# A gated attention and mixture-of-experts block: the passage from the GRU to the experts without GpSimd arithmetic

## The reference

```python
x = x + tanh(g_xattn[0]) * xattn(layernorm(x), ctx, ...)      # 3 GRU iterations
h = layernorm(x)
scores = sigmoid(h @ gate_w.T)
topk_score, topk_ids = top_k(scores.T, cap)
xin = h[topk_ids]
eo = (silu(xin @ gw + gb) * (xin @ up_w + up_b)) @ down_w + down_b
out = zeros.at[topk_ids].add(eo * topk_score)
shared = (silu(h @ sh_gate) * (h @ sh_up)) @ sh_down
x = x + tanh(g_ffn[0]) * (out + shared)
```

## Time and profile before

| | |
|---|---|
| median of 3 runs | 1204.84 us (1204.55 to 1205.53) |
| profiled execution | 1202.21 us, its span 1200.5 us |
| busy: TensorE, VectorE, ScalarE, GpSimd | 1114.3 (93%), 820.7 (68%), 559.2 (47%), 436.6 us (36%) |
| granted TensorE clock, mean | 0.959 |
| HBM traffic over the span | 76 GB/s |

### The profile page before, as it was taken

The page is one execution under the profiler, slowest core; times in us unless marked ns, Lnnn a source line. Parts: engine busy times, 40 slices in busy tenths (PEclk is TensorE's granted clock), DMA queues, the critical chain, the costliest instruction groups (busy, mean ns, idle before and its releaser), DMA issues. The chain is left out here.

```text
span 1200.5 us, 18388 instructions
## 1 busy us (share of the span) xinstructions
PE 1114.3 (93%) x6174; PEld 964.1 (80%) x6174; DVE 820.7 (68%) x1552; ACT 559.2 (47%) x839; POOL 436.6 (36%) x334
## 2 busy tenths in 40 slices
PE   5659999999999787999988999999999999999996
PEld 3548888888888566888876888888888888888896
DVE  7575878787865986778864666566666665666663
ACT  4243545544546466232334554455555544555542
POOL 5232444344411733343541232243323423343332
PEclk9659999999999899999998999999999999999999
DMA  4310011010104234001045434454444334544421
GB/s 158 97 36 1 3 34 25 11 35 0 35 1 127 67 106 133 22 17 35 18 143 178 117 96 127 136 141 94 125 133 135 96 123 140 141 95 124 133 37 18
DMA packets 47525, 98.75 MB, mean 82 GB/s; under 512 B 11392, under 2 KB 37248, under 8 KB 43136
## 3 DMA queue, kind: packets, MB, share of 16 engines
q1 hardware_dynamic: 33728, 79.13, 20.4%
q0 software_dynamic: 12288, 17.31, 8.5%
q10 hardware_dynamic: 1472, 1.84, 0.4%
HBM read 74.11 MB, written 17.07 MB: 76 GB/s over the span
## 5 line engine op out<-in xcount | busy, mean ns | idle before, releaser
L2067 DVE SCALAR_TENSOR_TENSOR hid<-wide,b_up,silu 128x512 f32<-128x512 f32 x120 | 90.1, 751 | 165.8 <-PE wide L1317 159.4
L956 POOL DMA_INDIRECT out_tokens<-y,idx_out x64 | 111.8, 1747 | 235.2 <-DVE y L2049 188.7
L1317 PE MATMUL wide<-xt_hi,w_hi 128*128 128x512 f32 x480 | 189.3, 394 | 3.1 <-DVE xt_lo L2032 3.1
L1317 PE MATMUL wide<-xt_lo,w_hi 128*128 128x512 f32 x480 | 188.6, 393 | 0.0
L1317 PE MATMUL wide<-xt_hi,w_lo 128*128 128x512 f32 x480 | 187.6, 391 | 0.0
L1619 ACT ACTIVATE silu<-wide,b_gate 128x512 f32<-128x512 f32 x120 | 82.1, 685 | 147.8 <-PE wide L1317 147.8
L1331 PE MATMUL down<-w_hi,hid_hi 128*128 128x256 f32 x480 | 136.6, 284 | 0.0
L1331 PE MATMUL down<-w_lo,hid_hi 128*128 128x256 f32 x480 | 135.9, 283 | 0.0
L1331 PE MATMUL down<-w_hi,hid_lo 128*128 128x256 f32 x480 | 135.7, 283 | 0.0
L1628 ACT ACTIVATE hid_hi<-hid 128x512 fp32r<-128x512 f32 x120 | 76.0, 633 | 101.1 <-DVE hid L2067 101.1
L2017 DVE TENSOR_TENSOR w_lo<-raw,w_hi 128x768 fp32r<-128x768 f32 x128 | 121.4, 949 | 0.0
(11 more groups left out here) (320 smaller groups left out, 2516.2 us busy)
## 6 DMA issues: line engine op xcount, KB each, us to landing
raw<-in_w_expert SPq DMA_DIRECT2D x32, 1536.0 KB, 6.7
work<-in_x SPq DMA_DIRECT2D x8, 512.0 KB, 4.7
token_rows<-work SPq DMA_DIRECT2D x8, 512.0 KB, 3.2
out_tokens<-y SPq DMA_DIRECT2D x8, 512.0 KB, 3.0
attn<-rms_c SPq DMA_DIRECT2D x24, 128.0 KB, 2.3
attn<-expo SPq DMA_DIRECT2D x24, 128.0 KB, 2.4
b_down<-in_down_b SPq DMA_DIRECT2D x1, 2048.0 KB, 12.5
sh_full<-in_w_shared SPq DMA_DIRECT2D x1, 1536.0 KB, 6.1
```

Source lines behind the costliest of these rows:

```text
L956: pool.indirect_dma_start(out, bass.IndirectOffsetOnAxis(idx_out[:, j:j + 1], 0), y[:, j, :], None, compute_op=ALU.add).then_inc(g_add, 16)
L1317: last = nc.tensor.matmul(bank[:, f % 2, :], w[f // HALF_F][:, f % HALF_F, (c + k) * P:(c + k + 1) * P], x_[:, k, :], start=(m == 1), stop ...
L2067: nc.vector.scalar_tensor_tensor(hid[:, f % 2, :], eup[:, f % 2, :], b_up[:, bass.ds(e, 1), f:f + 1].rearrange("p a b -> p (a b)"), silu[: ...
```

## The change

GpSimd leaves the arithmetic of the transition and of the later shared blocks:

- VectorE adds x for all eight groups, with the gate's factor, straight from PSUM; `copy_x` goes.
- The low part of groups 0 to 4 is formed in PSUM: TensorE adds `slots_hi` times minus one (`neg_i`) onto the turned bank (`subtract_hi`), and ScalarE copies what is left (`low`). Groups 5 to 7 are on VectorE. `turn_h` becomes a matmul with accumulate flags.
- The statistics' chains run over 3, 2, 2 and 1 groups. The first shared block moves behind the router, turns and x loads are in another order.
- The bisection holds only `cand`; the bits come from two small tables that GpSimd fills with 64 one-column memsets.
- From block 18 on VectorE takes the low parts, and from group 4 on it adds to y.
- Half of the id writes are issued by ScalarE; SyncE stores y(6) earlier, and loads the second half of expert 0 and `b_down` only after the gather has landed; `b_down` has its own semaphore, waited on in `results`.

```diff
@@ TensorE
+                            last = nc.tensor.matmul(h_banks(g)[:, k, b * P:(b + 1) * P], hg[:, g % 2, b, k * P:(k + 1) * P],
+                                                    ident[:, :], start=(b == 0), stop=(b == BLK - 1), is_transpose=True,
+                                                    skip_group_check=True)
...
+                def subtract_hi(g):
+                    pe.wait_ge(a_hh, g + 1)
+                    for k in range(KC):
+                        last = nc.tensor.matmul(h_banks(g)[:, k, :], neg_i[:, :], slots_hi[:, k, group_of(g)],
+                                                start=False, stop=True, skip_group_check=True)
+                    last.then_inc(m_sub, 1)
...
                 gru_unit(LAST, 1, 0, 0)
-                turn_slots(2, (a_xs, 1))
-                turn_slots(3, (a_xs, 2))
                 gru_unit(LAST, 1, 0, 1)
+                turn_slots(2, (v_x1, 1))
+                turn_slots(3, (v_x1, 2))
                 gru_unit(LAST, 1, 1, 0)
                 gru_unit(LAST, 1, 1, 1)
-                turn_slots(4, (a_xs, 3))
+                turn_slots(4, (v_x1, 3))
                 gru_unit(LAST, 1, 2, 0)
-                turn_h(0, (a_xs, 4))
-                gru_unit(LAST, 1, 2, 1)
-                turn_slots(5, (v_x1, 1))
-                turn_h(1, (a_hf, 1))
-                gru_unit(LAST, 1, 3, 0)
-                turn_h(2, (a_hf, 2))
-                gru_unit(LAST, 1, 3, 1, lambda: turn_slots(6, (v_x1, 2)))
-                turn_h(3, (a_xs, 5))
+                turn_h(0, (v_x1, 4))
+                pe.wait_ge(p_neg, 3)
+                gru_unit(LAST, 1, 2, 1, lambda: subtract_hi(0))
+                turn_slots(5, (v_x1, 5))
+                turn_h(1, (a_hlo, 1))
+                gru_unit(LAST, 1, 3, 0, lambda: subtract_hi(1))
+                turn_h(2, (a_hlo, 2))
+                def middle():
+                    subtract_hi(2)
+                    turn_slots(6, (v_x1, 6))
+                gru_unit(LAST, 1, 3, 1, middle)
+                turn_h(3, (v_x1, 7))
@@ ScalarE
+                gru_unit(LAST, 1, 2, 0, None, steps((normalise_x1, 1)), steps((high, 0), (normalise_x1, 2)))
+                gru_unit(LAST, 1, 2, 1, None, steps((low, 0)), steps((high, 1), (normalise_x1, 3)))
+                gru_unit(LAST, 1, 3, 0, None, steps((low, 1)), steps((high, 2), (normalise_x1, 4)))
+                gru_unit(LAST, 1, 3, 1, None, steps((low, 2)))
+                high(3)
...
+                        if (g, f) == (G - 2, FS - 2):
+                            act.wait_ge(v_ids, 1)
+                            for q in range(1, E // BLK, 2):
+                                act.dma_start(idv[:, :, q, :], ids_sb[:, q, :]).then_inc(w_ids, 16)
@@ VectorE
-                gru_group(LAST, 1, 0, (lambda: first_x1(0, 1),), (lambda: first_x1(2, 3),))
-                gru_group(LAST, 1, 1, (lambda: chain(0),), (lambda: chain(1),))
-                gru_group(LAST, 1, 2, (lambda: first_x1(4),), (lambda: first_x1(5),))
-                gru_group(LAST, 1, 3, (lambda: chain(2),))
-                first_x1(6)
+                gru_group(LAST, 1, 0, (lambda: first_x1(0, 1),), (lambda: first_x1(2),))
+                gru_group(LAST, 1, 1, (lambda: first_x1(3), lambda: chain(0)))
+                gru_group(LAST, 1, 2, (lambda: first_x1(4), lambda: chain(1)), (lambda: first_x1(5),))
+                gru_group(LAST, 1, 3, (lambda: first_x1(6), lambda: chain(2)))
...
-                    nc.vector.tensor_scalar(keep[:, :], small[:, 0:1], float(CAP), -1.0, ALU.is_ge,
+                    nc.vector.tensor_scalar(keep[:, :], small[:, 0:1], float(CAP), bit_f[:, bass.ds(u, 1)], ALU.is_lt,
                                             ALU.mult).then_inc(v_bis, 1)
...
+                    nc.vector.scalar_tensor_tensor(cand[:, :], keep[:, :], bit_i[:, bass.ds(u, 1)], cand[:, :],
+                                                   ALU.bitwise_or, ALU.bitwise_xor).then_inc(v_bis, 1)
...
+                def late_hidden(n):
+                    if n > OWN_LO:
+                        own_low(n - 1)
+                    hidden(n, n % FS, n < OWN_LO + 2)
@@ SyncE
+                for q in range(0, E // BLK, 2):
                     sp.dma_start(idv[:, :, q, :], ids_sb[:, q, :]).then_inc(w_ids, 16)
...
-                sp.wait_ge(m_ids, HALVES)
+                store_y(G - 2)
+                sp.wait_ge(g_in_, 16 * BLK)
                 sp.dma_start(raw[:, HALF_F:FE, :], w_expert[0, :, HALF_F:FE, :]).then_inc(l_w[1], 16)
```

More of the change, by code:

```diff
@@ L190, in flamingo_kernel @@
         rtmp2 = small_place("rtmp2", [P, G * BLK])
-        thr = small_place("thr", [P, 1], I32)
-        bit = small_place("bit", [P, 1], I32)
         cand = small_place("cand", [P, 1], I32)
@@ L795, in _ @@
                 sp.wait_ge(v_ids, 1)
-                idv = ids.rearrange("(q f) (a b) -> a f q b", f=BLK, b=BW)
-                for q in range(E // BLK):
+                for q in range(0, E // BLK, 2):
                     sp.dma_start(idv[:, :, q, :], ids_sb[:, q, :]).then_inc(w_ids, 16)
@@ L873, in _ @@
                 nc.gpsimd.memset(same_e[:, :], 0.0).then_inc(p2, 1)
-                add_x(0)
-                add_x(1)
-                add_x(2)
-                add_x(3)
+                nc.gpsimd.memset(neg_f[:, :], 0.0).then_inc(p_neg, 1)
+                for u in range(32):
+                    nc.gpsimd.memset(bit_f[:, u:u + 1], float(1 << (29 - u)) if u < 30 else 0.0)
+                    last = nc.gpsimd.memset(bit_i[:, u:u + 1], 1 << (28 - u) if u < 29 else 0)
+                last.then_inc(p_bit, 1)
+                pool.wait_ge(p_neg, 1)
+                nc.gpsimd.affine_select(out=neg_f[:, :], in_=neg_f[:, :], compare_op=ALU.not_equal, fill=-1.0,
+                                        base=0, pattern=[[-1, P]], channel_multiplier=1).then_inc(p_neg, 1)
+                pool.wait_ge(p_neg, 2)
+                nc.gpsimd.tensor_copy(neg_i[:, :], neg_f[:, :]).then_inc(p_neg, 1)
                 for f in range(FS):
@@ L1549, in scale_sums @@
                                          scale=tanh_g[:, 1:2]).then_inc(a_y, 1)
-                def later(step, g):
-                    return lambda: step(g)
                 act.sem_inc(a_silu, 2)
@@ L1831, in chain @@
                 def chain(q):
-                    own = slice(2 * q * BLK, 2 * (q + 1) * BLK)
-                    dve.wait_ge(v_st, 2 * BLK * (q + 1))
-                    for t in range(2 * q * BLK, 2 * (q + 1) * BLK):
+                    first, last = CHAINS[q][0] * BLK, (CHAINS[q][-1] + 1) * BLK
+                    own = slice(first, last)
+                    dve.wait_ge(v_st, last)
+                    for t in range(first, last):
                         st.add(nc.vector.bn_aggr(mv2[:, t, :], stats2[:, t, :]))
@@ L1867, in _ @@
                 last.then_inc(v_norm, 1)
-                for g in range(SUB_POOL, G):
+                for g in range(SUB_PE, G):
                     dve.wait_ge(a_hh, g + 1)
@@ L1875, in _ @@
                 st.add(nc.vector.memset(ones[:, :], 1.0))
-                st.add(nc.vector.memset(thr[:, :], 0))
-                st.do(nc.vector.memset(bit[:, :], 1 << 29))
+                st.do(nc.vector.memset(cand[:, :], 1 << 29))
                 dve.wait_ge(p2, 3 + 2 * G + 4)
@@ L1882, in _ @@
                 st.add(nc.vector.tensor_scalar(own_e[:, :, :], own_e[:, :, :], part_f[:, :], None, ALU.is_equal))
+                dve.wait_ge(p_bit, 1)
                 dve.wait_ge(a_sg, 1)
                 def bisect_count(u):
-                    nc.vector.tensor_scalar(cand[:, :], bit[:, :], thr[:, 0:1], None, ALU.bitwise_or).then_inc(v_bis, 1)
-                    dve.wait_ge(v_bis, 3 * u + 1)
                     nc.vector.tensor_scalar(slot[:, :], sg[:, :], cand[:, 0:1].bitcast(F32), 0.0, ALU.is_ge, ALU.add,
@@ L1921, in _, with own_low, own_y @@
                         bisect_keep(u + 1)
-                thr_f = thr[:, 0:1].bitcast(F32)
+                def own_low(n):
+                    dve.wait_ge(a_hid, n + 3)
+                    nc.vector.tensor_tensor(hid_lo[:, n % FS, :], hid[:, n % 2, :], hid_hi[:, n % FS, :].bitcast(F32),
+                                            ALU.subtract).then_inc(v_lo, 1)
+                def late_hidden(n):
+                    if n > OWN_LO:
+                        own_low(n - 1)
+                    hidden(n, n % FS, n < OWN_LO + 2)
+                def own_y(g):
+                    dve.wait_ge(a_y, g + 2)
+                    plus_x1(nc.vector, g)
+                thr_f = cand[:, 0:1].bitcast(F32)
                 n = G_BIS * FS + LAG
@@ L1931, in _ @@
                 dve.sem_inc(v_tot, 1)
-                hidden(n, 0)
+                late_hidden(n)
                 dve.wait_ge(m_tot, 1)
@@ L1942, in _ @@
                 dve.sem_inc(v_tot, 1)
-                hidden(n + 1, 1)
+                late_hidden(n + 1)
                 dve.wait_ge(m_tot, 2)
@@ L1997, in _ @@
                         planes_a(i, part)
```

(7 more changed lines are left out.)

212 lines of the change are left out of this document (90 added, 122 removed).

## The result

| | before | after |
|---|---|---|
| median of 6 runs | 1204.69 us | 1199.89 us |
| all runs | 1203.85 to 1205.53 | 1193.70, 1194.34, 1199.71, 1200.07, 1200.56, 1200.82 |
| ratio after / before, 95% interval | | 0.9949 (0.9935 to 0.9962) |
| profiled execution | 1202.21 us, span 1200.5 | 1194.34 us, span 1192.6 |
| busy: TensorE, VectorE, ScalarE, GpSimd | 1114.3, 820.7, 559.2, 436.6 us | 1113.3, 812.6, 553.6, 387.2 us |

The changed kernel is faster, by 0.51%, less than half of what was forecast, and its runs fall into two groups 6 us apart, which those of the kernel before don't do. Two executions at a lower mean clock (1405 us in experiment 5 at 0.742, 1856 us of the kernel before at 0.555) are left out everywhere.

A forecast was written before the change was run, and what follows sets the result against it. TensorE was taken to bound the kernel, with its waits in transition, bisection and hand-off to win. Terms 3.4+1.7+0.3+7.7 = 13.1 us off the 1204.84 median gave 1191.7 us (0.45), range 1186.5 to 1200.

The forecast's parts named there:

- Transition, −3.4: From the last GRU iterations to the first bisection count: a walk of the new order gave 472.5 against 475.9 before.
- The bound of −6: Transition's most favourable bound: −6 us if half-clock time shrinks too; the other bound was +3.6.
- Bisection, −1.7: Two one-column steps fewer per candidate, 0.44 with gaps; 0.3 to 0.5 gained per pass, four passes; range 0 to −3.
- That addition and its stretch stay: Bisection: GpSimd's addition to y keeps stretching `thr` to 1.63, with the next count 0.91 late, once in each pass.
- First scan, −0.3: Shorter bisection steps were to save 0.3 us more from the first scan.
- hand-off, −7.7: Hand-off to the experts: earlier ids, quicker id writes and an unqueued gather, with the 1.8; range −4 to −10.
- the −1.3 for the id writes: Hand-off: SyncE and ScalarE issue two id writes each; the four took 2.53 before, so 1.3 us less.
- The gather's 3.9: Hand-off: with queues nearly free, last gather issue to TensorE's release takes 2.8 to 2.9 instead of 6.8.
- Late blocks, ids 1.8 earlier: Late shared blocks: VectorE takes 12.0 us more, loses about 11 of GpSimd's stretch; no TensorE wait, `ids_sb` 1.8 earlier.
- ScalarE's stand at 0.3: ScalarE stands for `v_ids` and two id-write issues, costing some 0.3 us at the end of the shared work.
- The rivals: Gather gains nothing, 0.18; VectorE binds transition, 0.15; clock stays full, 0.10; late blocks stay stretched, 0.05; half clock slows transition, 0.07.
- GpSimd's 64 fills: Small table fills from 375 on, 13 us, or 40 at three times the step; wanted later, so they cost nothing.

The follow-up runs named there:

- experiment 5: Changed kernel, with GpSimd's third `sh_lo` waiting until VectorE has ended the `pre` of half 0 of the unit behind it; 1196.5 us, one group.
- experiment 10: Kernel before the change, with `thr` taken as a per-partition scalar, so one tensor input less in the step that keeps a bit; 1201.35 us, ratio 0.9974.
- Experiments 2: Changed kernel with the old bisection (`thr`, `bit` and `cand` as before), the rest changed; 1192.4 us, ratio 0.9891.
- 3: Changed kernel, with the bisection's last step taking `cand` as a per-partition scalar, one tensor input less; 1188.8 us, ratio 0.9871.
- 6: Changed kernel, with GpSimd's low part of a bisection block waiting for the end of the block's second candidate; 1191.3 us, ratio 0.9891.
- 12: Kernel before the change, with the new bisection alone (one candidate, bits from two tables); 1210.8 us, ratio 1.0060.
- experiment 11: Kernel before the change, with SyncE's new order of loads alone; 1200.0 us, ratio 0.9955.
- (4): Changed kernel with SyncE's old order of loads: second half of expert 0 and `b_down` before the first gather; 1204.05 us.
- experiment 9: Changed kernel with one-input last bisection step and later third `sh_lo`, but late low parts and y additions mostly back on GpSimd; 1189.7 us, ratio 0.9875.
- the kernel with both repairs: Changed kernel with one tensor input in the bisection's last step and the later third `sh_lo` together; 1184.7 us, ratio 0.9837.

## Why the forecast was wrong, by its own steps

- **Transition, −3.4.** Right for two runs in three, in size and in its steps: −3.0 to the first count in the slower group, where the two `pre` that the walk had ending at 404.3 and 411.9 end at 404.12 and 411.89. The other group has −7.1, by an accident of the clock that takes `sh_lo` out of VectorE's way. My walk had two steps stretched by `sh_lo`; it didn't ask what happens if TensorE is late. The bound of −6 was too near for that group.
- **Bisection, −1.7: this step failed.** It said that the steps that remain "take their bit from a table by a register, which I price at 0 to 0.2", and that "the pass gains what the shorter steps give". The two steps start 0.12 and 0.14 later than the old ones and the first is 0.06 longer, 0.3 and not 0 to 0.2, so little of the 0.44 was left to gain. And it would have gained little anyway: the removed steps stood where they cost nothing, since experiment 10 shows the old four hidden behind TensorE once the y encounter is gone. What counted was when the two-input step comes: by 0.42 us later it fell onto the start of `hid_lo`, took 1.3 and not 0.22 in 15 of 16 blocks, and made a block 5.37 long and not 4.62. The sentence "That addition and its stretch stay" was wrong too: `cand` ran past the addition to y. I had read that two-input instructions of VectorE end just behind the GpSimd instruction that they meet, had used it in the transition and the late blocks, and didn't lay the new times of `cand` beside those of `hid_lo`: the earlier trace rows show only the step beside the addition to y, and I took that one encounter of the loop for all there could be. Experiments 2, 3, 6 and 12 show it each from another side: the old steps, one input less, no encounter, and the new steps alone.
- **First scan, −0.3, and hand-off, −7.7.** Near in the sum (−6.9 in the slower group), with one term that isn't there. In that group's profile the first id write comes 2.3 sooner behind the scan (49.90 and 52.17; forecast 1.8 and 0.3). From the gather's last issue to the turn are 3.10 and not 6.82, 3.7 less (forecast 3.9). From the turn to the first expert are 3.80 and not 5.06, as forecast. But the −1.3 for the id writes failed: from SyncE's first id write to its read-back are 4.29 (3.78 in the quicker group), and 3.79 before. Half the writes on ScalarE left SyncE's queue sooner, and the read-back still waited for all four. The gather's 3.9 measured 4.3 alone (experiment 11) and 4.8 taken back (4). The figure of the Trainium skill that I weighed against the 3.9 ("DMA: Bandwidth & Descriptors", Latency and other measured facts) would have given 1.8 by estimate; the runs decide for the rows.
- **Late blocks, ids 1.8 earlier.** Right in size (2.3 above, 2.1 in experiment 9). About half of it, 1.1, is the step that writes `ids_sb`, which takes 0.20 and took 1.27. In the kernel with both repairs it is worth 3.7 in its stage, because ScalarE's id writes and GpSimd's gather hang on the same events. I had priced ScalarE's stand at 0.3 and not tied it to the term that makes it small. In the changed kernel TensorE waits 0.44 for `y` there in the slower group's profile; the 1.42 of the quicker one (617.82) goes with two id writes of ScalarE that took 2.50 there and 1.52 in the other.
- **The rivals.** None of the five had the bisection: each was about the transition, the gather, the clock or the late blocks. GpSimd's 64 fills, which I bounded by 13 to 40 us, took 2.1 (376.01 to 378.09) and cost nothing either way.

The Trainium skill ("SBUF — State Buffer", Who interferes with whom) says that a VectorE instruction with two SBUF inputs contends with a GpSimd instruction that reads SBUF, that whichever is issued first holds the pair of ports for its whole duration, and that one SBUF input outside the two-port modes doesn't contend. The traces agree in three points. A step with two inputs that starts beside a `hid_lo` lasts as long as that does (1.32 and 1.29), one that starts 0.24 us or more ahead of it takes 0.22, and one with a single SBUF input takes 0.27 beside it. They agree the other way round too: in the quicker group `pre<-tr,hb` started 0.31 ahead of `sh_lo` and kept its 0.69, and a `sh_lo` took 2.09 there, where the others took 1.8. On the order within less than that they don't decide: the starts of the 15 stretched steps are recorded from 0.05 ahead of `hid_lo`'s to 0.02 behind it, and VectorE is the one held up in all. The rule should have sent me to compare the times of `cand` and `hid_lo`. Whether the loss could have been read ahead of the run is not shown, since it hangs on 0.42 us that no row of the kernel before gives.

## What to carry to other kernels

When instructions of an engine are shortened or given another operand form in a loop that three engines share, write down where each two-input VectorE step will then start against GpSimd's, within a tenth of a microsecond: an encounter costs what is left of the other instruction however small the step is (1.1 us more for a step of 0.22 here), and in this loop it came back in 15 of 16 blocks. Take the second tensor input out of small steps first (a one-column tensor can be a per-partition scalar): here it was worth 2.9 us in the kernel before and 10.4 in the changed one, and the new steps, two hidden ones fewer and two operands by register, cost 6.6. And if the runs of a kernel fall into two groups, compare a trace of each before judging the change: here a wait on an event (experiment 5) made one group out of two.

## What the runs showed of the hardware

- A VectorE step on one column whose scalar operand has its address in a register started 0.12 to 0.14 us later behind the step it waits for than its predecessor with a fixed address (0.43 against 0.31, 0.34 against 0.20); `keep` ran 0.22 instead of 0.16, the two-input step 0.22 in both. The operations changed with the addresses, and no run separates the two.
- Two executions of one program had TensorE's clock differently behind equal waits: eight transposes in 1.06 or 1.86 behind 1.69 us, and the stretch behind the scan granted 1.00 or 0.70 behind 1.64 or 1.66. What decides that stays open. Behind the scan it moved the time by some 1 us directly. In the transition half clock made the first count 4.1 us earlier, through the order of GpSimd and VectorE.
- A VectorE step with one input, the one that writes `ids_sb` (128x64, uint32 from f32), took 1.27 and 1.26 beside a `hid_lo` of GpSimd and 0.20 without; 16 digit planes in f16, one input too, took 4.90 and 6.09 and not 2.27. So one input was no protection for these; no row tells in which mode they ran. The bisection's step with one input, on int32 columns, was not held up (0.27).
